# Row sums by source in the count matrix stage of a four-layer graph network: trios of four columns for pairs of eight

## What is computed

```python
messages_fwd = _calc_messages(H, E, ht[:, 0], W_fwd, b_fwd)
messages_back = _calc_messages(H, E, ht[:, 1], W_back, b_back)
msg_dst = jnp.concatenate([ht[:, 1], ht[:, 0]])
messages = jnp.concatenate([messages_fwd, messages_back], axis=0)
agg = jax.ops.segment_sum(messages, msg_dst, num_segments=n)
counts = jax.ops.segment_sum(jnp.ones((msg_dst.shape[0],)), msg_dst, num_segments=n)
...
x = _layernorm(x + _L0_gnn_ref(x, L0_gnn_W, L0_gnn_b, src, dst), axis=-1)
x = _layernorm(x + _L1_gnn_ref(x, edge_attr_128, edge_index_t, ...), axis=-1)
```

## Time and profile before

| | us |
|---|---|
| median of 3 runs | 8362.07 |
| lowest and highest run | 8346.99, 8362.63 |
| span of the profiled execution | 8349.1 |
| of it: edges listed and sorted | 232.5 to 1373 |
| of it: count matrix, its loop | 1455 to 2980 |
| of it: the layers | 2980 to 8349.1 |

### The profile page before, as it was taken

One profiled execution on the slowest core, in us unless ns is written; L12 is line 12 of the kernel. 1 busy time (PEld: TensorE's weight loads), 2 busy tenths in 40 slices (PEclk: granted clock), 3 DMA queues, 4 the chain that ended last, 5 costly groups with the idle time before them and its releaser, 6 DMA issues. The chain is left out here.

```text
span 8349.1 us, 148737 instructions
## 1 busy us (share of the span) xinstructions
PE 6017.2 (72%) x38749; PEld 4203.0 (50%) x38788; DVE 4413.6 (53%) x11592; ACT 2264.1 (27%) x5042; POOL 3509.7 (42%) x3566
## 2 busy tenths in 40 slices
PE   0266620666667669999995777767777759996899
PEld 0255510444444335555554677756777735553455
DVE  6877772666776632312225777777777740103311
ACT  0322200443344320100002555535555510000100
POOL 0677787566666400000004777747777700000400
PEclk6688865988999889999997999989999979998899
DMA  0122201222222446677672222212222236664566
GB/s 17 39 70 70 71 18 27 94 89 94 91 95 95 80 126 173 181 187 183 165 187 67 55 55 54 55 48 55 54 55 55 54 96 193 187 196 126 138 194 180
DMA packets 835093, 849.38 MB, mean 102 GB/s; under 512 B 417843, under 2 KB 779026, under 8 KB 828243
## 3 DMA queue, kind: packets, MB, share of 16 engines
q1 hardware_dynamic: 710533, 561.67, 24.6%
q0 software_dynamic: 115904, 201.65, 10.9%
q10 hardware_dynamic: 8208, 80.51, 2.4%
HBM read 665.89 MB, written 97.31 MB: 91 GB/s over the span
## 5 line engine op out<-in xcount | busy, mean ns | idle before, releaser
L1923 POOL DMA_INDIRECT d_row_ring<-table_att,src_at x1664 | 1579.2, 949 | 642.7 <-issue 486.5
L2545 PE MATMUL psum<-e_a_ring,e_parts 128*128 128x448 bf16 x6174 | 1184.5, 353 | 76.8 <-DVE e_parts L2659 76.8
L777 POOL DMA_INDIRECT b_row_ring<-edge_attr,b_entry x896 | 895.6, 1000 | 590.7 <-SPq L754 350.5
L796 PE MATMUL psum<-b_hot 128*128 x2872 | 650.6, 366 | 567.5 <-DVE b_hot L981 435.9
L354 POOL DMA_INDIRECT listed<-a_record,a_slot_no x832 | 866.1, 1041 | 315.2 <-issue 272.5
L2545 PEld LDWEIGHTS psum<-e_a_ring,e_parts 128*128 128x128 bf16 x6174 | 605.1, 98 | 632.9 <-issue 81.3
L1332 PE MATMUL psum<-c_a_ring,c_parts 128*128 128x448 bf16 x4116 | 812.9, 356 | 47.5 <-DMA c_a_ring<-adjacency 42.9
L1948 PE MATMUL psum<-edges_out,edges_in 128*128 128x120 f32 x4896 | 691.7, 300 | 158.4 <-ACT edges_in L2014 157.2
L1948 PEld LDWEIGHTS psum<-edges_out,edges_in 128*128 128x128 f32 x4896 | 641.1, 211 | 204.2 <-issue 204.2
L796 PEld LDWEIGHTS psum<-b_hot 128*128 x2872 | 283.2, 99 | 908.2 <-issue 784.3
L981 DVE TENSOR_SCALAR b_hot<-b_iota,b_key_dst 128x896 int16 x1436 | 679.7, 473 | 4.4 <-issue 4.0
(11 more groups left out here) (469 smaller groups left out, 8110.8 us busy)
## 6 DMA issues: line engine op xcount, KB each, us to landing
e_a_ring<-adjacency SPq DMA_DIRECT2D x1029, 224.0 KB, 2.8
c_a_ring<-adjacency SPq DMA_DIRECT2D x686, 224.0 KB, 2.9
adjacency<-b_line ACTq DMA_DIRECT2D x49, 1568.0 KB
a_cum<-edge_attr SPq DMA_DIRECT2D x103, 512.0 KB
d_row_ring<-table_att,src_at POOLq DMA_INDIRECT x1664
b_row_ring<-edge_attr,b_entry POOLq DMA_INDIRECT x896
listed<-a_record,a_slot_no POOLq DMA_INDIRECT x832
e_a_left<-adjacency_left SPq DMA_DIRECT2D x28, 224.0 KB, 3.3
```

Source lines behind the costliest of these rows:

```text
L777: pool.indirect_dma_start(out=row_ring[:, u % 4, g, 0:D], out_offset=None, in_=a["edge_attr_128"], in_offset=bass.IndirectOffsetOnAxis(ap= ...
L796: mm = nc.tensor.matmul(ps[:, v, :], four[:, half, j, 0:P], four[:, half, j, P + v * WIN:P + (v + 1) * WIN], start=False, stop=True, skip_ ...
L1923: pool.indirect_dma_start(out=row_ring[:, u % 4, g, :], out_offset=None, in_=table_att[layer], in_offset=bass.IndirectOffsetOnAxis(ap=src_ ...
L2545: mm = nc.tensor.matmul(psum[:, 2 * (turn % 2) + v, 0:WIN], (few_parts if d == 2 else parts)[:, piece, s, :], a_ring[:, (FIRST[turn] + s) ...
```

## The change

Row sums by source go by units of four columns ("quads", 224 of them) and not of eight. Three pairs (tile, quad) make a `trio`: each pair has four float32 matmuls into its own third of one PSUM bank, and two trios alternate between two banks. Every line has two trios, one ahead of cell 3 and one ahead of cell 0 of the next line; the table TURN is gone. There are 97 trios, 291 places for pairs, where there were 81 twos, 162 places. PE waits for DVE's additions once a trio (s_added), and DVE waits for the sums once a trio (s_sum). Each line PE loads six codes and DVE twelve; SP loads eight words of `out_end` for four units, of which it uses every second. The tables are made over 224 quads, with four passes in place of eight for `column_key`; some of their arrays lie in memory that other arrays had. The gathers stay units of eight columns in a ring of four.

```diff
-    TWOS = (UNITS + NT + 1) // 2
+    QUAD, TRIO = 4, 3
+    QUADS = COLS // QUAD
...
-    TURN = (2, 2, 1, 2, 2, 1)
-    TURN_TWOS = sum(TURN)
+    LINES = 6
+    TRIOS = NT // LINES * 2 * LINES + 1
...
-    QI, QJ = -(-(NB * NT + 1) // P), 2
+    QI, QJ = -(-(NB * NT + 1) // P), 3
...
                 for k in range(2):
                     st.settle(dve)
-                    st.by(V.tensor_tensor(column_ended, bc(columns[:], 1, [P, UNITS, NT]),
-                                          bc(all_columns[:, :, k * (G - 1)], 2, [P, UNITS, NT]), ALU.is_le))
+                    st.by(V.tensor_tensor(column_ended, bc(columns[:], 1, [P, QUADS, NT]),
+                                          bc(all_columns[:, :, k * (QUAD - 1)], 2, [P, QUADS, NT]), ALU.is_le))
...
-                for g in range(G):
-                    st.by(V.tensor_tensor(column_ended, bc(columns[:], 1, [P, UNITS, NT]),
-                                          bc(all_columns[:, :, g], 2, [P, UNITS, NT]), ALU.is_le))
+                for g in range(QUAD):
+                    st.by(V.tensor_tensor(column_ended, bc(columns[:], 1, [P, QUADS, NT]),
+                                          bc(all_columns[:, :, g], 2, [P, QUADS, NT]), ALU.is_le))
...
-            is_src = sbb("is_src", [P, 2, 2, G, P])
+            row_quads = row_ring[:].rearrange("p u (b g) f -> p (u b) g f", g=QUAD)
+            is_src = sbb("is_src", [P, 2, TRIO, QUAD, P])
...
-            ps_row = [psum[:, 6 + k, 0:D + 1] for k in range(2)]
+            ps_row = [[psum[:, 6 + k, h * (D + 1):(h + 1) * (D + 1)] for h in range(TRIO)] for k in range(2)]
...
-                    done = loaded(sp, out_end[0:1, bass.ds(i * 4, 4)], 9)
+                    done = loaded(sp, out_end[0:1, bass.ds(i * 8, 8)], 9)
                     for u in range(4):
-                        hold(sp, s_sum, done[u], s_held_sp)
+                        hold(sp, s_sum, done[2 * u + 1], s_held_sp)
...
-                def two(i, parity, pair):
-                    for h, (_, unit) in enumerate(pair):
-                        hold(pe, s_rows, unit + 1, s_held_pe)
-                        pe.wait_ge(s_is_src, i * 2 + (h + 1))
-                        pe.wait_ge(s_added, i * 2 + (h + 1))
-                        for c in range(G):
-                            mm = nc.tensor.matmul(ps_row[h], is_src[:, parity, h, c, :],
+                def trio(i, parity, pairs):
+                    for h, (_, quad) in enumerate(pairs):
+                        hold(pe, s_rows, (quad >> 1) + 1, s_held_pe)
+                        pe.wait_ge(s_is_src, i * TRIO + (h + 1))
+                        if h == 0:
+                            pe.wait_ge(s_added, i * TRIO + TRIO)
+                        for c in range(QUAD):
+                            mm = nc.tensor.matmul(ps_row[parity][h], is_src[:, parity, h, c, :],
...
-                        units = codes_of(pe, out_pairs, UNITS - 1, i * (2 * TURN_TWOS) + 2 * m, 2 * twos)
+                        pairs = codes_of(pe, out_pairs, QUADS - 1, (i * (2 * LINES) + m) * TRIO, 2 * TRIO)
...
-                        two(i * TURN_TWOS + m, m % 2, units[0:2])
+                        trio(i * (2 * LINES) + m, 0, pairs[0:TRIO])
                         cells(s, 3, NWIDE, before)
-                        if twos == 2:
-                            two(i * TURN_TWOS + (m + 1), (m + 1) % 2, units[2:4])
+                        trio(i * (2 * LINES) + (m + 1), 1, pairs[TRIO:])
                         cells(s + 1, 0, 3, before[NWIDE - 3:])
...
-                def add(i, h, code):
+                def add(i, parity, h, code):
                     at = bass.ds(code[0], 1)
-                    dve.wait_ge(s_sum, i * 2 + (h + 1))
-                    hold(dve, s_added, i * 2 + (h + 2), s_held_dve)
+                    if h == 0:
+                        dve.wait_ge(s_sum, i * TRIO + TRIO)
+                    hold(dve, s_added, i * TRIO + (h + 2 * TRIO), s_held_dve)
```

More of the change, by code:

```diff
@@ L210, in gnn_kernel @@
             span_i = sbb("span_i", [P, 2, NB], I32)
[L211 to L214, removed]
+            tile_span = rank[:, 0:2 * QUADS].rearrange("p (k u) -> p k u", k=2)
+            ones_n = rank[:, 2 * QUADS:3 * QUADS]
+            tiles_n, pair_end, shift_by = (scratch[:, k * QUADS:(k + 1) * QUADS].bitcast(F32) for k in range(3))
             even = sbb("even", [P, 1], I32)
@@ L535, in _ @@
                     st.settle(dve)
[L536 removed]
+                    st.by(V.tensor_tensor_scan(pair_end[:, 0:n], ones_n[:, 0:n], tiles_n[:, 0:n], 0.0, ALU.mult, ALU.add))
                     st.settle(dve)
@@ L819, in two @@
                         mm.then_inc(s_sum, 1)
                 cells(0, 0, 3, befores(pe, 0, 4))
-                with pe.Fori(0, NT // len(TURN)) as i:
-                    for k, twos in enumerate(TURN):
-                        s, m = i * len(TURN) + k, sum(TURN[:k])
-                        units = codes_of(pe, out_pairs, UNITS - 1, i * (2 * TURN_TWOS) + 2 * m, 2 * twos)
-                        before = befores(pe, i * (len(TURN) * NWIDE) + (k * NWIDE + 3), NWIDE + 1)
-                        two(i * TURN_TWOS + m, m % 2, units[0:2])
+                with pe.Fori(0, NT // LINES) as i:
+                    for k in range(LINES):
+                        s, m = i * LINES + k, 2 * k
+                        pairs = codes_of(pe, out_pairs, QUADS - 1, (i * (2 * LINES) + m) * TRIO, 2 * TRIO)
+                        before = befores(pe, i * (LINES * NWIDE) + (k * NWIDE + 3), NWIDE + 1)
+                        trio(i * (2 * LINES) + m, 0, pairs[0:TRIO])
@@ L987, in cells, with codes @@
                         cell(s, slice(w * WIDE, (w + 1) * WIDE), spans[w - first])
-                def codes(q, n):
-                    return codes_of(dve, out_pairs, UNITS - 1, q, n)
+                def codes(trio, n):
+                    return codes_of(dve, out_pairs, QUADS - 1, trio * TRIO, n * TRIO)
                 def hot_of(parity, h, code):
-                    tile, unit = code
-                    V.tensor_tensor(is_src[:, parity, h, :, :], bc(key_src[:, bass.ds(unit * G, G)], 2, [P, G, P]),
-                                    bc(iota[:, bass.ds(tile * P, P)], 1, [P, G, P]), ALU.is_equal).then_inc(s_is_src, 1)
@@ L1001, in add, with turned_over @@
                     V.tensor_tensor(edges_out[:, at, :].rearrange("p a f -> p (a f)"),
-                                    edges_out[:, at, :].rearrange("p a f -> p (a f)"), ps_row[h], ALU.add
+                                    edges_out[:, at, :].rearrange("p a f -> p (a f)"), ps_row[parity][h], ALU.add
                                     ).then_inc(s_added, 1)
-                def turned_over(i, parity, pair, later):
-                    for h in range(2):
-                        add(i, h, pair[h])
+                def turned_over(i, parity, pairs, later):
+                    for h in range(TRIO):
+                        add(i, parity, h, pairs[h])
@@ L1008, in turned_over @@
                         hot_of(parity, h, later[h])
                 for i in range(2):
-                    for h, code in enumerate(codes(2 * i, 2)):
+                    for h, code in enumerate(codes(i, 1)):
                         hot_of(i, h, code)
                 cells(0, 0, 3, spans_of(dve, 0, 3))
[L1014 to L1018, removed]
+                with dve.Fori(0, NT // LINES) as i:
+                    for k in range(LINES):
+                        s, m = i * LINES + k, i * (2 * LINES) + 2 * k
+                        pairs = codes(m, 4)
+                        spans = spans_of(dve, i * (LINES * NWIDE) + (k * NWIDE + 3), NWIDE)
@@ L1025, in _ @@
                 cells(NT - 1, 3, NWIDE, spans_of(dve, (NT - 1) * NWIDE + 3, NWIDE - 3))
-                for h, code in enumerate(codes(2 * TWOS - 2, 2)):
-                    add(TWOS - 1, h, code)
-                dve.wait_ge(s_added, 2 * TWOS + 2)
+                for h, code in enumerate(codes(TRIOS - 1, 1)):
+                    add(TRIOS - 1, 0, h, code)
+                dve.wait_ge(s_added, TRIO * TRIOS + 2 * TRIO)
                 st.by(V.tensor_reduce(most[:], edges_out[:, 0:NT, D], AX_X, ALU.max))
```

32 lines of the change are left out of this document (17 added, 15 removed).

## The result

| | median us | ratio to before, 95% interval |
|---|---|---|
| kernel before (with the runs beside the changed one) | 8355.67 | |
| changed kernel | 8448.55 | 1.0117 (1.0102 to 1.0132) |

What follows compares the result with a forecast made beforehand. PE, mostly its sequencer, was taken to set the pace, with the supply of rows close behind. Terms 14 - 10 + 21 + 26 + 4 + 8 = +63 us on the median 8362.1 gave 8425 us, range 8355 to 8475.

Steps and rivals of the forecast that it cites:

- Tables, +14: First stage: two table passes of double width hold up POOL's scatters, with small extras; +14 us, between +6 and +17.
- Matmuls, -10: Row sums on PE: trios have 264 fewer matmul records, but sequencer steps limit the gain; -10 us, bounds -41 and +19.
- Groups, +21: In 16 of 48 lines a group is added between cell 6 and cell 0, 1.3 us each; +21 us, bounds 0 and +59.
- loads, +26: PE's six code words each line, ahead of the first group, take 0.55 us longer; +26 us, between +10 and +42.
- Their sign in the prediction: PE's wait before the row sums, shown as "issue", was to grow by 26 us or more.
- Supply of rows, +8: Gathered units at 12.25 us each give 31.7 us a line, where PE wants about 32; +8 us, bounds 0 and +30.
- rows become the bound: Rival: a gather unit takes 12.7 us on average, adding 35 us to the forecast, 8460 us; chance 0.17.
- DVE, +4: DVE's wait for all three pairs of a trio may delay one-hots that PE needs; +4 us, bounds 0 and +20.
- the clock, 0: Line's first groups on PE start at a low clock after gaps, but the array catches up by the third cell; 0 us.

Runs made afterwards that it cites:

- rows early: SP frees a ring place before waiting for the unit just gathered to land: kernel before with this edit 8304.66 us, changed kernel with it 8372.77 us.

## Why the prediction came out as it did

8425 was predicted, 8448.55 measured, within 8355 to 8475, and "slower" was right. Point by point:

**Tables, +14.** Right: the stage ends 14.46 us later, and scatters beside the wider pass take 11.19 us for 6.50. By the run with the tables made twice the two passes make all of it; the 2.5 us put on the last pass and the pair list don't show. The Trainium skill agrees: "SBUF — State Buffer", in "SBUF: two separate sides", says that DVE and GpSimd share one pair of ports as an exclusive lock, held for a whole instruction, for a DVE instruction with two inputs in SBUF against a GpSimd instruction that reads SBUF. The trace fits it: the scatter beside DVE's comparison, which reads two tables, takes as long as that pass, while scatters beside the sum of the same length behind it (L526, 11.59 us) take 0.96 us.

**Matmuls, -10.** The size was about right, the place was not. Behind a middle trio the next cell begins after 3.66 us for 3.67, and in the median of all whole middle groups after 3.59 (35 of them) for 3.68 (29). That is little, since the sequencer's steps take as long for 24 records as for the 32 of the earlier trace rows, 1510.6 to 1513.2:

```profile
L819 PEldq FUSED_REGOPS  x12: 46/46/52, 1524.6 to 1527.2; - x12
```

More came from the first groups of lines. Windows of one of them (columns as in rows 11) and its third cell, before and then after:

```profile
1861.29:1867.97 6.68, 6.68 (x33) 6.60 (x34) 3.35 (x11) 0.00 (x0) 3.61 (x5) 0.56 0.20 49
1871.19 1.74 PE L796 MATMUL psum<-b_hot 128*128 x8 [0.20 <-issue]
...
2123.06:2128.58 5.52, 5.52 (x25) 5.41 (x26) 4.47 (x16) 0.00 (x0) 3.03 (x4) 0.50 0.20 51
2132.23 1.74 PE L798 MATMUL psum<-b_hot 128*128 x8 [0.57 <-issue]
```

Both ran at a low granted clock (0.50 is the lower level, 1.2 GHz, throughout), and the third cell comes 9.90 us after the start of the two and 9.17 after that of the trio. Over all whole first groups it is 9.60 us in the mean before (45) and 9.33 after (42), with rows early 9.58 (48) and 9.25 (48). That is 0.3 us in each of 49 lines, some 13 to 16 us.

**Groups, +21, and loads, +26.** By the timelines the price of a group was right: from the cell ahead of a middle group to the cell behind it the median is 6.21 us before (29 twos) and 6.17 after (34 trios), and from cell 6 to cell 0 with none between 4.89 (16, before), so 1.3 us in each of 16 lines. No run has this term alone. The loads were right where PE sets the pace, 25 to 29 us with rows early. Their sign in the prediction, 26 us more of "issue" ahead of the row sums, did not come behind late rows (6 us more); with rows early the longer loads raise it from 174.5 to 204.5 us. PE's loads now have a least and a most of 798 and 1492 ns, where 0.86 and 1.56 us were worked out:

```profile
L169 DVEq TENSOR_LOAD <-tables x49: 769/871/2758, 1474.4 to 3066.2; - x49
...
L169 PEldq TENSOR_LOAD <-tables x49: 798/841/1492, 1476.4 to 3050.8; - x49
```

With rows early, the changed kernel stands 68 us over the kernel before with rows early (8372.77 and 8304.66); the sum without the term of the rows was 55. But in the kernel as it is, the two terms lie behind late rows until line 43 and in full only in the lines after. So that the number fell within the range is in part luck: 41 of its 63 us were charged to PE's own work in every line, which in this kernel sets the pace only in the last few.

**Supply of rows, +8: the step that failed.** It priced a unit by one step of 12.25 us; the mean was 13.1 to 13.3. The place of the rows in the argument was wrong too: they "stand close behind" PE, whereas they were ahead of it already. Late rows cost 46 us in the kernel before (by the run with rows early) and 76 in the changed one, at the least, since PE still waits 19.0 and 37.6 us for rows there. So the term was 30 us and not 8, the upper end that the text gave it, and perhaps near 50, if the 18.6 us by which those waits differ are counted too. 55 and 30 would have been 85 of the 93 measured. The rival "rows become the bound" had the mechanism and nearly the time (8460), with a chance of 0.17 for the 0.47 of the forecast, whose own upper end (8445) the result just passed. The 53.7 us of PE's waits were read as a small cost. They were what showed of a difference between two nearly equal paces: 13.27 us a unit from the rows, and 12.7 that PE takes when rows come early (the step from 1470.94 to 2827.83), some 60 us over 108 units. Where a line then uses 7% more units, 2.59 for 2.41, such a difference grows at once.

**DVE, +4, and the clock, 0.** DVE's loads of codes go up to 2.76 us as worked out, and nothing shows its slack used up. The cells' matmuls by line, the idle time before them and its releasers, of before and then of the changed kernel:

```profile
L796 PE MATMUL psum<-b_hot 128*128 x2856 | 645.2, 365 | 558.4 <-DVE b_hot L981 426.8 <-issue 81.6 <-ACT b_line L864 28.6
...
L798 PE MATMUL psum<-b_hot 128*128 x2858 | 644.5, 365 | 222.8 <-DVE b_hot L983 146.9 <-issue 52.5 <-ACT psum L856 14.7
```

Of the 426.8 us before, 321.9 are the first cell's lead-in, which the second stretch leaves out: 236 us of idle time before cells became 223. More of it is named for DVE (105, then 147), but in gaps of about 1 us that other names had. Ahead of the row sums, too, PE's waits named for DVE rose, from 14.3 to 37.3 us in all, while the gap ahead of a middle group stayed at 0.75 and then 0.77 in the median. No run changed DVE's side alone, so its term is not measured.

The clock's 0 rested on one pair of groups, and it held in the changed kernel only. In the kernel before, the third cell comes 9.86 us (median) behind the 12 first groups with a granted clock under 0.6, 9.39 behind the 25 between 0.6 and 0.75, and 9.36 behind the 8 at 1.00 (2.4 GHz): half a microsecond is lost behind the coldest. In the changed kernel all 42 whole first groups run under 0.75, and the third cell comes at 9.15 behind the 18 under 0.6 and 9.29 behind the rest. The Trainium skill's warning ("TensorE: Matmul & The Clock Gate", "HAM oscillation") so holds in part of the lines before, and costs the shorter trios nothing that shows.

**Open.** After the loop the changed kernel and its three variants took 5364.6 to 5381.2 us, the kernel before and its variants 5343.7 to 5364.8, with the same code. Some 10 us may lie there. The cause was not looked for.

## What to carry to other kernels

An engine with few and short waits for a producer is no proof of slack: look at what the producer's own queue waits for, and take the mean of its steps, not one of them. A ring of four places gives no overlap if the engine that frees places also waits for each landing before it frees the next; move that wait one turn back. And spread work that depends on a slow supply over the whole loop: used faster than it comes, it stalls the first lines and leaves the last ones without anything to overlap.

## What the runs showed of the hardware

From a unit's last gather to the release of the next unit, with the way over SP in it, it took about 2.1 us at the least and 3.2 in the mean (POOL's waits in both kernels). Where the gather ended within 12 us after ScalarE's issue of a line's 1.5 MB write, it was 4.0 us in the mean before (44 steps) and 3.7 after (40), at other times 2.8 in both (64 and 68). That the write is the cause was not tested. The Trainium skill, "DMA: Bandwidth & Descriptors", in "Anatomy of one DMA — SWDGE (gpsimd) path", gives about 2 us as the fixed cost of such a transfer, mostly until it is confirmed to have landed; the shortest waits agree with it, the mean here does not. On POOL, four loads of one word into a register cost some 2.5 us a unit in all, more than twice the 1.0 us that the rows of PE and DVE had let expect.
